# Attention block on one core: every stage from the first key's product on is moved one slot nearer to the query's product

## What is computed

```python
def reference(x, Wqkv, bqkv, Wproj, bproj, Wffn, bffn):      # x: 8 x 2048 x 512
    xn = layernorm(x)
    q, k, v = split(xn @ Wqkv.T + bqkv)                      # 16 heads of 32, each 8 rows x 2048 x 512
    scores = mask + scale * einsum("bnd,bmd->bnm", q, k)     # over the 8 rows n, m, apart for each b and head
    attn = softmax(scores) @ v
    lin = fp8(xn) @ fp8(Wffn).T + bffn
    return x + (attn @ Wproj.T + bproj) + lin
```

## Time and profile before

| | |
|---|---|
| median of 3 runs (lowest, highest) | 1527.31 us (1526.89, 1527.63) |
| the profiled execution: its time, its span | 1526.15 us, 1524.4 us |
| PE busy; weight loads | 1493.7 us (98%); 690.5 us (45%) |
| DVE busy | 1452.7 us (95%) |
| POOL busy | 1309.7 us (86%) |
| ACT busy | 1258.5 us (83%) |
| mean granted TensorE clock | 0.996 |

### The profile page before, as it was taken

How to read it: one execution, slowest core, us unless ns; L and a number is a source line. 1 busy time by engine, 2 the same in 40 slices (tenths; PEclk the granted TensorE clock), 3 DMA queues, 4 the chain that set the end, 5 groups by cost and what they waited for, 6 DMA issues and landing times.

```text
span 1524.4 us, 24286 instructions
## 1 busy us (share of the span) xinstructions
PE 1493.7 (98%) x6864; PEld 690.5 (45%) x6989; DVE 1452.7 (95%) x1220; ACT 1258.5 (83%) x2959; POOL 1309.7 (86%) x1027
## 2 busy tenths in 40 slices
PE   6999999999999999999999999999999999999997
PEld 3444444444444444444444444444444444444454
DVE  6999999999999999999999999999999999999897
ACT  5678889797888979889797888979889797887942
POOL 2588998999899989998999899989988999899884
PEclk9999999999999999999999999999999999999999
DMA  7444554545455454454545455554554545445432
GB/s 226 90 100 102 136 119 116 131 116 139 109 118 136 110 123 120 124 122 117 126 115 137 110 118 133 114 122 119 124 124 115 126 117 137 109 118 126 93 104 69
DMA packets 363414, 183.30 MB, mean 120 GB/s; under 512 B 311056, under 2 KB 311056, under 8 KB 363280
## 3 DMA queue, kind: packets, MB, share of 16 engines
q1 hardware_dynamic: 363280, 181.75, 49.5%
HBM read 73.41 MB, written 33.55 MB: 70 GB/s over the span
## 4 chain that ended last, share of the span: by engine, by line
PE 84%; POOL 3%; issue 3%; DVE 2%; DMA 0%; ACT 0%; SPq 0%; POOLq 0%; DVEq 0%; ACTq 0%
PE k_ps L943 19%; PE proj_ps L943 19%; PE q_ps L943 19%; PE v_ps L943 19%; PE lin_ps L985 6%; PE proj_ps L976 2%; POOL prod_pv L568 1%; DVE prod_qk L1184 1%; DVE scores L1189 1%; POOL prod_pv L626 1%; PE q_ps L1062 0%; POOL xs L555 0%; ACT prod_pv L681 0%; DVE q_ps L1301 0%; DMA oT<-o 0%
## 5 line engine op out<-in xcount | busy, mean ns | idle before, releaser
L568 POOL TENSOR_TENSOR prod_pv<-kv,probs 128x2048 f32<-128x2048 f32 (+1 forms) x182 | 612.0, 3363 | 9.6
L1189 DVE TENSOR_REDUCE scores<-prod_qk 128x64 f32<-128x2048 f32 x192 | 439.3, 2288 | 6.8 <-DVE prod_qk L1184 0.2
L1279 DVE TENSOR_REDUCE o_nat<-prod_pv 128x512 f32<-128x2048 f32 (+1 forms) x121 | 404.6, 3344 | 31.8 <-ACT prod_pv L681 19.3
L1184 DVE TENSOR_TENSOR prod_qk<-q_ps,kv 128x1536 f32<-128x1536 f32 (+1 forms) x192 | 397.9, 2072 | 0.2 <-issue 0.2
L943 PE MATMUL k_ps<-wqkv_hi,xT 128*128 128x512 f16 x1024 | 326.5, 380 | 1.4 <-DMA xT<-x 1.4
L943 PE MATMUL v_ps<-wqkv_hi,xT 128*128 128x512 f16 x1024 | 325.4, 379 | 0.0
L943 PE MATMUL q_ps<-wqkv_hi,xT 128*128 128x512 f16 x1024 | 325.4, 379 | 0.0
L943 PE MATMUL proj_ps<-wproj_hi,oT 128*128 128x512 f16 x952 | 302.6, 379 | 0.0
L681 ACT ACTIVATE prod_pv<-kv,probs 128x32 f32<-128x32 f32 x960 | 244.4, 340 | 0.0
L793 ACT ACTIVATE kv<-v_ps 128x512 f32<-128x512 f32 x128 | 140.7, 1099 | 86.5 <-PE v_ps L943 86.4
L943 PE MATMUL k_ps<-wqkv_lo,xT 128*128 128x512 f16 x512 | 195.1, 381 | 0.0
(11 more groups left out here) (173 smaller groups left out, 2035.0 us busy)
## 6 DMA issues: line engine op xcount, KB each, us to landing
xn<-in_L_attn_x SPq DMA_DIRECT2D x132, 256.0 KB, 2.8
xs<-in_L_attn_x SPq DMA_DIRECT2D x124, 256.0 KB, 2.6
out<-xs SPq DMA_DIRECT2D x124, 256.0 KB, 2.1
xT<-x SPq DMA_TRANSPOSE x256, 3.0
kv<-in_L_attn_Wqkv SPq DMA_DIRECT2D x3, 1024.0 KB, 8.2
oT<-o SPq DMA_TRANSPOSE x122, 3.2
kv<-in_L_attn_Wproj SPq DMA_DIRECT2D x1, 1024.0 KB, 5.9
prod_pv<-in_L_ffn_weight SPq DMA_DIRECT2D x1, 1024.0 KB, 10.0
```

The source lines that it names most:

```text
L568: nc.gpsimd.tensor_tensor(o, v, p, ALU.mult).then_inc(pv_multiplied, 1)
L1184: nc.vector.tensor_tensor(prod_qk[:, 1:1 + m0 + 4 - m1, :], qb, k, ALU.mult).then_inc(qk_multiplied, 1)
L1189: nc.vector.tensor_reduce(scores[:, n % 2, :, m0:m0 + 4].rearrange("p h m -> p m h"), prod_qk[:, row:row + 4, :].rearrange("p m (h d) -> p ...
L1279: nc.vector.tensor_reduce(o_nat[:, n % 2, :], prod_pv[:, place:place + units, :].rearrange("p q (c m) -> p c q m", m=4), AX_XY, ALU.add).t ...
```

## The change

The nine lags from `L_FIRST` to `L_PROJ` and the one of `L_RES` become smaller by one: `L_FIRST` 6, `L_QK` 7, `L_SHIFT` 8, `L_SOFT` 9, `L_PV` 10, `L_SUM` and `L_RES` 11, `L_SPLIT` 12, `L_LIN` 13, `L_PROJ` 14. The lags up to `L_Q` stay. So tile n's scores are taken in slot n+7, two slots behind its q. There are 132 slots, and the q of the last tile, which belonged to slot 132, stands in the ending, behind the projection of tile 118 and the linear layer of tile 119.

```diff
 L_STATS, L_CENTRE, L_NORM, L_KV, L_Q, L_FIRST, L_QK, L_SHIFT, L_SOFT, L_PV, L_SUM, L_RES, L_SPLIT, L_LIN, L_PROJ = \
-    1, 2, 3, 4, 5, 7, 8, 9, 10, 11, 12, 12, 13, 14, 15
+    1, 2, 3, 4, 5, 6, 7, 8, 9, 10, 11, 11, 12, 13, 14
...
-ENDING = TILES + 5
+ENDING = TILES + 4
...
                 copy_query(t - 2)
+                preset_q(0, t - 1)
...
             def ending():
                 t = TILES
+                late_projection(t - 10)
                 late_linear(t - 9)
-                late_projection(t - 10)
+                pe.wait_ge(q_preset, TILES)
+                split_products(q_ps[(t - 1) % 4], xT[:, (t - 1) % XT, :, :], wqkv_hi, wqkv_lo, 0,
+                               first=False).then_inc(q_summed, 1)
                 sum_unit(t - 7, 0)
```

## The result

Median 1535.52 us (1534.09 to 1536.71) against 1526.94 us (1526.75 to 1527.63) of the kernel before, five runs of each: ratio 1.0054 (95% interval 1.0043 to 1.0065). Forecast were 1533.8 us, 1527.8 to 1539.0, and slower with a chance of 0.76. The profiled execution took 1534.09 us, its span is 1532.3 us: 7.9 us longer than before, where 6.6 were forecast. DVE's busy time is nearly what it was (1455.3 us for 1452.7). PE's reads 1501.1 us for 1493.7, but the two can't be compared: the trace of before lacks 125 of the 6989 matmul records that this one has. What PE waits is better compared. Its listed waits from 80 us on sum to 13.6 us now and to 7.0 before.

A forecast was written before the change was run, and what follows sets the result against it. PE's computing sets the middle's pace, DVE close behind. The end moves S - 5.05: S of 9.8 gives +4.7, the clock +1.9, together +6.6: span 1531, time 1532.7, plus 1.16 to the median: 1533.8 us, range 1527.8 to 1539.

The forecast's parts named there:

- First wait: Slot 10: the late output-bias addition delays POOL, x and its transposing DMA, so PE waits 4.24 us before k.
- Slots 11 to 17: Head: DVE starts slot 15 at 133.9; k of slot 17 follows at least 21.99 us later; waits total 9.8 us.
- The clock: PE's slot 10 wait drops the clock, +1.9 us; a second fall (+1.9) and a spared tail fall (-1.9) cancel.
- The middle: DVE waits for k instead of ACT's products, within 1.07 us a group, without slowing PE: cost 0, thin cover.
- S: All waits of PE after the change, slots 8 to 131: 9.8 us, 11.7 with the clock's fall.
- case 3: Middle overflows: DVE's new waits for k exceed 1.07 us a group; each 1 us over costs 14 us; 8%.
- The tail: Tile 124's second unit follows the last k's copy by 0.1 us instead of 7.88; the remaining 65.7 us stay fixed.
- S - 5.05: Movement of the kernel's end in us, from 3.67 - 0.94 + S - 7.78; slower if S exceeds 5.05.
- My anchor: Tail: 65.7 us from tile 124's second unit to the span's end, taken as fixed before and after.
- PE's lateness in the ending: Ending: with the last q still to do, PE is 4.1 us later against DVE, taken as hidden by idle time.
- rivals 1 and 2: Head: first wait covered, S below 2.0, faster, 7%; no change that can be told, S 2.0 to 8.1, 15%.
- Rival 4: Middle: PE makes its waits good, only DVE's lateness counts, the end moves +1.1 us to 1528.4; 2%.

The follow-up runs named there:

- e1: The change, with DVE's addition of the output biases moved ahead of tile 1's unit (slot 8): median 1530.36 us, ratio 1.0022 to the kernel before.
- e2: The kernel before, with only DVE's addition of the output biases moved to the end of slot 9: median 1533.97 us, ratio 1.0047.
- e7: The change, with POOL's cutting of the output biases into rows moved from the start of slot 9 to its end: median 1534.54 us, ratio 1.0047.
- e9: The change, with the last tile's query first in PE's ending, ahead of the projection of tile 118 and linear layer of tile 119: 1536.26 us, ratio 1.0059.
- e3: The change, with POOL's low half of x ahead of shift, low half of o and rstd, and SP's DMAs of x ahead of o's: 1532.88 us, ratio 1.0032.
- e4: The change with the diffs of e1 and e3 together: median 1526.44 us (11 runs), ratio 0.9997 to the kernel before.
- e10: The change again without any edit, on the chip of e9: 1536.45 us, ratio 1.0060 to the kernel before.
- e5: e4, with DVE's softmax sums ahead of the first unit in slots 15 and 16 alone: median 1525.97 us (11 runs), ratio 0.9993.
- e8: e5, with the store of tile 122 in SP's ending moved behind the last transposing DMA of o: median 1526.10 us (11 runs), ratio 0.9993.
- e6: The kernel before, at its old lags, with only e3's order on POOL and SP: median 1525.99 us (11 runs), ratio 0.9991.

## Why the prediction was right, point by point

- **First wait.** Right in every link: line 1267 at 67.97 (forecast 67.76), the first cast at 68.72 (68.5), the low half of x at 76.01 (75.80), the wait 4.04 (4.24; the terms stated add up to 4.19). e1 takes it away, e2 makes it alone.
- **Slots 11 to 17.** Right. Tile 4's second unit at 94.21 (92.3, and 1.9 for the clock), slot 15 at 135.89 (133.9 + 1.9). DVE, a slot ahead in its list, waits 4.98 us for k there and gains nothing tile for tile. The rule taken from one pair of rows, 21.99 us, gave 21.95 to 21.97 in six other traces (the change twice, e1, e2, e7, e9); where e3's order shortened its path it gave 19.23 twice (e3, e4).
- **The clock.** Right in the profiled execution as to the first fall: k takes 80.42 to 84.70 there, 4.28 us for 2.59, so 1.7 for the 1.9 forecast (no row that the forecast shows gives its 8 or 9 slow matmuls). As a rule ("should do the same") it was too firm. Waits of 3.82 (e3, slot 10) and 2.62 us (the change, slot 17) were followed by none, 2.66 (e1, slot 17) and 2.65 us (e10, slot 17) by one. "I let these two cancel" did not hold as meant. In the profiled execution neither fall came, which by the forecast's own terms is 1.9 us in the change's favour; the tail used it up by other things (below), and that is luck. In e10 both came, and five of its six runs lie at 1536.3 us or above, where the profiled execution of the change took 1534.1.
- **PE's busy time.** "Some 10 us less between 60 and 155" was wrong: 5.1. The four waits before 155 sum to 6.2 us; that of slot 17 lies behind it (155.2 to 157.8), and the slow matmuls count as busy.
- **The middle.** Cost 0 forecast; 0.8 us measured: from k of slot 17 to the last k are 1304.9 us, 114 slots of 11.44 make 1304.2, and S came out at 12.5 for 11.7. It stands in three places: k of slots 19, 26 and 33 starts 0.18, 0.31 and 0.28 us late, each behind a late xT (the last at 341.66). So the thin cover of 0.6 us a group was short by up to 0.3 us in the first groups; from there on k comes every 11.44 us, and case 3 is out. DVE waited 12.7 us for k there and none for last-key products.
- **The tail.** From tile 124's second unit to the end 66.1 for 65.7, but the way there is not as forecast: two errors met. The transposing DMA of o of tile 124 landed in 4.58 us instead of 3.08, DVE's subtraction (line 1361, before 1357) ended 0.66 later, and so PE's matmuls behind that DMA started 2.2 us later, counted from tile 124's second unit. From them to the last residual it was 1.7 us shorter, as the clock did not fall (9.27 us for 10.97). In five executions where it fell (e3, e4, e5, e8, e10) the whole way takes 67.6 to 68.0 us, in e7 68.8. In the profiled executions this is why e4 and e5 don't come out under the kernel before by the 1.9 and 2.5 us that S - 5.05 gives them (S of 3.2 and 2.5). My anchor was one execution's value: e6, at the old lags, shows 67.8.
- **PE's lateness in the ending.** "I take that as hidden" was too much: 0.7 of the 4.1 us came through. ACT's copy of tile 127's q stands behind its work on PE's results. It started 14.11 us behind tile 124's second unit before and 18.23 now, 4.1 later; POOL waited 2.94 us for it, and POOL's last product before the subtraction came 0.67 us later. The subtraction ended with that product, as the last section shows. Before (two rows of ACT and POOL), and after:

```profile
1472.83 0.59 ACT L805 ACTIVATE q_first<-q_ps 128x512 f32<-128x512 f32 x1
...
1487.83 3.64 POOL L626 TENSOR_TENSOR prod_pv<-kv,probs 128x2048 f32<-128x2048 f32 x1
```

```profile
1484.42 0.59 ACT L805 ACTIVATE q_first<-q_ps 128x512 f32<-128x512 f32 x1
...
1485.08 1.27 POOL L549 TENSOR_TENSOR prod_qk<-q_first,kv 128x512 f32<-128x512 f32 x1 [2.94 <-ACT q_first L805]
```

- **The balance S - 5.05.** It holds for the last copy of k, e5: 1455.49 is 5.25 behind 1450.24, so S = 2.5, and its listed waits are 1.9 plus some 0.17 for each restart of PE. With S = 12.5 in the change, rivals 1 and 2 (S up to 8.1) are out. What was left out is the spread of the tail.
- **Rival 4** (PE makes its waits good) is out: at full clock matmuls start 0.216 us apart in every trace, after a wait as before it. The Trainium skill's 131 ns a matmul (TensorE: Matmul & The Clock Gate, Back-to-back issue gap) is not reached in any of them; its value for an isolated one, some 216 ns, is what a full slot shows.
- **The size.** 1533.8 forecast, 1535.5 measured: of the 1.7 us 0.8 lie in the middle, 0.4 in the tail, and some 0.3 in the distance from the profiled execution to the median, which was 1.43 us and not 1.16. That the size came out so near is in part the luck of the tail.

## What to carry to other kernels

When a stage is moved nearer by a slot, ask first what bounds it in the stretch where no queue is filled yet: a consumer that is bound by its own work gains nothing there. What it hands back (here its sums, with POOL's and SP's work queued behind them) can then bind the engine that was free. A path measured once in the trace, from a slot's start on one engine to the instruction on another that waited for it, is worth more than a sum of its parts: it held in six other traces to 0.05 us. One-time work in a slot of a running pipeline (the output biases) costs by what is queued behind it, on each engine and queue it crosses. Moving its source forward took the wait away (e1); moving a later part of it back only moved the wait (e7). Last, a lateness that "idle time will hide" has to be followed through the engines that copy its results: 0.7 of 4.1 us came through in the change, and more in e9.

## What the runs showed of the hardware

**DVE waits out a GpSimd instruction.** The subtraction in line 1361 reads two tensors, both in SBUF. It took 0.29 us before, 0.90 in the change, 2.26 in e9; the same shapes each time. POOL's product that ran beside it, in the change:

```profile
1495.97 3.64 POOL L626 TENSOR_TENSOR prod_pv<-kv,probs 128x2048 f32<-128x2048 f32 x1
```

It ends at 1499.61 and the subtraction at 1499.75; in e9 1501.81 and 1501.96; before, it started at 1487.83 and ended at 1491.47, the subtraction (1491.33, 0.29 us) at 1491.62. In all twelve traces DVE is done 0.14 to 0.16 us behind POOL's end, however long before it began. A second instruction shows it with a measure of what it takes undisturbed: line 1305, with both inputs in SBUF, takes 0.21 us when it starts with nothing under way on POOL, and 3.44 beside POOL's products (two in one row here), ending 0.10 us behind the second:

```profile
1500.16 0.21 DVE L1305 TENSOR_TENSOR q_ps<-exps,inv_sum 128x64 f32<-128x64 f32 x1
...
1504.78 7.24 POOL L626 TENSOR_TENSOR kv<-kv,probs 128x2048 f32<-128x2048 f32 x2
...
1508.68 3.44 DVE L1305 TENSOR_TENSOR q_ps<-exps,inv_sum 128x64 f32<-128x64 f32 x1
```

DVE's products of query and keys, which read the query from `q_ps` in PSUM, are not held: they take 2.23 to 2.29 us with POOL's products beside them or not. The Trainium skill (SBUF — State Buffer, Terms) says of the port pair that the two share that it is held for the full instruction and the other blocks; the traces agree with it for these two instructions. Such an instruction's duration is a wait in disguise, with no idle time shown.

**The clock after a wait.** Equal waits of PE (2.6 to 4 us) are followed by the lower level, 1.2 GHz, in one execution and not in another of nearly the same program: in slot 17 with 2.62 none (the change), with 2.61, 2.65 and 2.66 one (e9, e10, e1); in slot 10 with 3.82 none (e3), with 4.03 and 4.04 one (e10, the change); in the tail with 3.55 and 3.63 none (e1, the change), with 2.54 and 3.47 one (before, e7). So the length of the wait alone does not tell. Nine falls in the head cost 1.4 to 1.7 us each, and they go with the spread of the runs (e3: 1529.6 to 1533.6). The Trainium skill (TensorE: Matmul & The Clock Gate, Part 1) says of the rise to full speed that its point varies from run to run; here it is the fall that varies.
